# Self-attention stage of a fused transformer layer: reordering VectorE and GpSimd within a tile's pass

## What is computed

```
x = x + cross_attention(layernorm(x), context)      # context 64 x 256 x 256, 16 heads of 16
x = x + causal_self_attention(layernorm(x))         # 16 heads of 16, 64 positions
x = x + ffn(layernorm(x))                           # 256 -> 1024, ternary weights, 8-bit activations
```

```
att = softmax(where(causal, q @ k.T / 4, -inf));   y = att @ v;   x + y @ w_out + b_out
```

## Time and profile before

| | us |
|---|---|
| median of 3 runs | 949.87 |
| lowest, highest | 948.79, 952.31 |
| profiled execution, own time | 948.79 |
| profiled execution, span of the instructions | 947.0 |
| PE busy | 888.6 (94%) |
| DVE busy | 790.7 (83%) |
| ACT busy | 690.9 (73%) |
| POOL busy | 344.8 (36%) |
| mean granted TensorE clock | 0.991 |

### The profile page before, as it was taken

The page is one execution under the profiler, slowest core; times in us unless marked ns, Lnnn a source line. Parts: engine busy times, 40 slices in busy tenths (PEclk is TensorE's granted clock), DMA queues, the critical chain, the costliest instruction groups (busy, mean ns, idle before and its releaser), DMA issues. The chain is left out here.

```text
span 947.0 us, 29217 instructions
## 1 busy us (share of the span) xinstructions
PE 888.6 (94%) x9714; PEld 722.3 (76%) x9730; DVE 790.7 (83%) x1711; ACT 690.9 (73%) x1983; POOL 344.8 (36%) x487
## 2 busy tenths in 40 slices
PE   5899999999999999999999988999999987999997
PEld 4788888888888888888888876878787863555554
DVE  3788878888888888887788877988888876999997
ACT  3587776776777767777677665777777765988887
POOL 1322322223222232224322337767666632222221
PEclk9999999999999999999999999999999997999999
DMA  9111111111111111111111000000000000000001
GB/s 303 37 39 39 43 34 40 40 39 34 39 39 44 39 34 39 39 44 39 34 39 39 28 1 2 1 2 0 1 0 1 2 1 1 28 28 28 28 28 39
DMA packets 31618, 31.64 MB, mean 33 GB/s; under 512 B 3280, under 2 KB 30800, under 8 KB 31568
## 3 DMA queue, kind: packets, MB, share of 16 engines
q1 hardware_dynamic: 30720, 30.73, 10.5%
q10 hardware_dynamic: 848, 0.33, 0.1%
HBM read 26.86 MB, written 4.19 MB: 33 GB/s over the span
## 5 line engine op out<-in xcount | busy, mean ns | idle before, releaser
L485 ACT ACTIVATE probs<-psum,nmax 128x256 f32<-128x256 f32 x512 | 237.8, 488 | 89.6 <-DVE nmax L445 89.6
L445 DVE TENSOR_REDUCE nmax<-psum 128x2 f32<-128x512 f32 x256 | 159.0, 684 | 30.8 <-PE psum L315 30.8
L328 PE MATMUL psum<-id_sb,probs 128*128 128x128 f32 x1024 | 136.4, 277 | 14.3 <-ACT probs L485 14.1
L328 PEld LDWEIGHTS psum<-id_sb,probs 128*128 128x128 f32 x1024 | 111.8, 141 | 30.3 <-ACT probs L485 29.2
L493 POOL TENSOR_TENSOR rstd<-vare,minus_half 128x1 f32<-128x1 f32 x96 | 52.9, 551 | 182.2 <-DVE vare L382 179.7
L502 POOL TENSOR_TENSOR cl<-c_sb,ch 128x512 fp32r<-128x512 f32 x64 | 81.7, 1276 | 99.8 <-ACT ch L460 99.8
L485 ACT ACTIVATION_READ_ACCUMULATOR probs<-psum,nmax 128x1 f32 x512 | 112.7, 220 | 0.0
L466 ACT ACTIVATE probsT<-psum 128x512 f32<-128x512 f32 x160 | 91.0, 625 | 9.0 <-PE psum L328 8.9
L509 POOL TENSOR_TENSOR rm<-rinv,hm_sb 128x256 f32<-128x256 f32 x64 | 39.8, 622 | 127.7 <-DVE rinv L421 127.7
L315 PE MATMUL psum<-k_sb,qb 32*128 32x256 f32 x1024 | 78.4, 404 | 0.0
L1006 PE MATMUL psum<-wb_all,xqT 128*128 128x512 bf16 x240 | 66.2, 390 | 10.3 <-DVE probs L906 7.0
(11 more groups left out here) (126 smaller groups left out, 2303.5 us busy)
## 6 DMA issues: line engine op xcount, KB each, us to landing
c_sb<-in_ctx_t SPq DMA_DIRECT2D x64, 256.0 KB, 2.7
x_sb<-in_x SPq DMA_DIRECT2D x32, 128.0 KB, 2.0
out<-y_sb SPq DMA_DIRECT2D x32, 128.0 KB, 1.7
w_all<-in_w_gate SPq DMA_DIRECT2D x1, 1024.0 KB, 7.9
w_all<-in_w_up SPq DMA_DIRECT2D x1, 1024.0 KB, 10.0
w_all<-in_w_down SPq DMA_DIRECT2D x1, 1024.0 KB, 12.5
wqkv_sb<-in_w_qkv SPq DMA_DIRECT2D x1, 768.0 KB, 6.3
wq_sb<-in_wq ACTq DMA_DIRECT2D x1, 256.0 KB, 3.9
```

Of the source, the lines that this page charges most:

```text
L328: last = nc.tensor.transpose(sp[g][:, c:c + P], probs[:, 2 * g + u, kh * P:(kh + 1) * P], id_sb[:])
L445: nc.vector.tensor_reduce(nmax[:, 2 * g:2 * g + 2], sp[g].rearrange("p (u s) -> p u s", u=2), AX.X, ALU.max, negate=True).then_inc(max_don ...
L485: nc.scalar.activation(probs[:, j, :], sp[g][:, u * S:(u + 1) * S], ACT.Exp, bias=nmax[:, j:j + 1], accum_out=rsum[:, j:j + 1]).then_inc(e ...
```

## The change

Two orders are changed, both in `body2`, and no instruction is added, removed or altered. On DVE, `dve_xn` of tile t + 6 moves ahead of `dve_sum2` of tile t + 1. On POOL, `pool_kbd4` of tile t + 2 moves ahead of `pool_rm2` of tile t, and `pool_xb2` of tile t + 6 moves ahead of `pool_xl` of tile t + 5.

```diff
@@ vector engine, body2
                     if t > 0:
                         dve_y2(v, t - 1)
+                    if t + 6 < NT:
+                        dve_xn(v, LN2, t + 6, at(t + 6), xt2_mm)
                     if t + 1 < NT:
                         dve_sum2(v, t + 1)
-                    if t + 6 < NT:
-                        dve_xn(v, LN2, t + 6, at(t + 6), xt2_mm)
                     if t + 2 < NT:
                         dve_v2(v, t + 2, t % 2)
@@ gpsimd, body2
                 def body2(t):
-                    pool_rm2(p, t)
                     if t + 2 < NT:
                         n = (t + 2) // 2
                         pool_kbd4(p, t + 2, n, n % 2, t % 2)
+                    pool_rm2(p, t)
                     if t + 6 < NT:
                         pool_rstd(p, LN2, t + 6)
+                        pool_xb2(p, t + 6)
                     if t + 5 < NT:
                         pool_xl(p, t + 5, (t + 5) // 2 % 2, (t + 5) % 2)
-                    if t + 6 < NT:
-                        pool_xb2(p, t + 6)
```

## The result

The changed kernel takes 958.57 us, the median of 8 runs (954.76 to 959.84), against 950.50 for the kernel before in its 8 runs (947.75 to 952.31). The ratio is 1.0089, with a 95% interval of 1.0075 to 1.0102: slower, by about 8.5 us, where no measurable change was forecast.

A forecast was written before the change was run, and what follows sets the result against it. PE was taken to bound the self-attention stage. Profiled execution 948.79 us + 0.55 for two late passes = 949.3; with the median 1.08 higher, 950.4 was stated, range 948.5 to 953.5, no measurable change.

The forecast's parts named there:

- What bounds the kernel: Self-attention stage, 600 to 760 us: it runs at PE's pace, PE busy 159.28 of 160.00 us.
- The DVE edit: `xn` before the row sum on DVE: waits about 0.11 us for `rstd`, with 0.22 of cover left; cost zero.
- third rival: DVE becomes late if the wait before `xn` passes 0.33: 2.7 us, 952.6; chance 0.82 together with the main forecast.
- The POOL edit: POOL's order: `xb2` lands in idle time, `kbd4` goes ahead of `rm2`; the whole 1.26 us slack is spent, about zero cost.
- The sum over POOL: From the split's start to PE's `r2` load: 3.24 us, against 3.28 available, so 0.04 early.
- first rival: `rm2` becomes PE's wait at L701 in every pass: at 0.20 late, 5.4 us, 955.3; chance 0.12.
- The two single late passes: PE's `r2` load late after the splits at 586.82 and 725.40: 0.29 + 0.26 = 0.55 us.
- The slow `xn`: Three `xn` on DVE of up to 0.89 us return to 0.33 in the new place; their 0.48 us isn't counted.
- The scores start earlier: Rival: holes before L678 and L671 are waits for `kbd4`; its earlier end returns up to 6.7 us, 943.2; chance 0.06.

The follow-up runs named there:

- e7: Kernel before with PE's five hardware-loop rounds (20 passes) written out, orders and buffers as before: 947.27 us, ratio 0.9947.
- e8: Changed kernel with two `xn` buffers used in turn and PE's hardware loop written out: 946.20 us, ratio 0.9936 to the kernel before.
- e1: Kernel before with only the DVE move, `xn` ahead of the row sum; POOL's order as before: 953.99 us, ratio 1.0029.
- e6: Kernel before with only the DVE move of `xn`, plus two `xn` buffers in this stage: 951.38 us, ratio 0.9995.
- e3: Changed kernel with `kbd4` put back behind `rm2`; `xn` and `xb2` stay moved: 954.69 us, ratio 1.0038 to the kernel before.
- e4: Changed kernel with two `xn` buffers used in turn, all three moves kept: 951.74 us, ratio 0.9999 to the kernel before.
- e5: Kernel before with one move alone, `kbd4` ahead of `rm2`; `xb2` and `xn` in their old places: 967.44 us, ratio 1.0165.
- e2: Kernel before with only the POOL moves, `kbd4` ahead of `rm2` and `xb2` ahead of the split: 973.16 us, ratio 1.0233.

## Why the prediction was wrong, point by point

- *What bounds the kernel*: right. PE sets the pace of this stage; e7 and e8 show it again from the other side, since less of PE's own time shortens every pass.
- *The DVE edit, "`rstd`, which `xn` needs, ends on POOL at 710.20, so DVE now waits about 0.11 us"*: this is the step that failed. `xn` has two waits, and the second, for PE's transpose of the tile before, was left out. `dve_xn` was priced by its input alone. With that transpose's load starting 2.02 us after PE's load and its matmul ending 2.46 after it, `xn` couldn't start at 1.84. The row was there to be used: the transpose at L631 in PE's timeline. It cost about 0.75 us of DVE in every pass. The queue behind it was listed rightly and its cover (0.22 us) too; a wait of 0.77 breaks through that cover, which is the third rival's mechanism, with a wait seven times the forecast 0.11 and over twice the 0.33 that the rival set as its condition. The prediction also had no loop in it: `y2` late makes PE's transpose late, and that makes `xn` late. e1 prices it: 2.8 us. e6 takes the missed wait away, and the step as written holds: `xn` starts 1.84 after the load, DVE's idle time before L733 falls from 0.33 to about 0.2, and the ratio is 0.9995.
- *The POOL edit, "`xb2` lands in what is now POOL's idle time and leaves the pair behind it"*: wrong in consequence. `xb2` waits for `xn`, and with `xn` at 2.53 it pushes the split, `kbd4` and `rm2`. `kbd4` ahead of `rm2` had used up the slack of 1.26 us, so nearly all that the split is late (0.42 us) is PE's (0.35 a pass). That is the rest of the loss, from e3's 1.0038 to 1.0089.
- *The sum over POOL, 3.24 us from the split to PE's load*: right. In the changed kernel it is 716.55 - 713.34 = 3.21, and in e4 it fits under 3.28 with no wait. In the kernel written out it fits under 6.42 too. So the first rival, that `kbd4` makes `rm2` late whatever `xn` does, had the right symptom (PE waits at L701, passes over 6.7 us) and the wrong cause: e4 has the same order and no such wait. Without `xn`'s and `xb2`'s move it is true, as e5 and e2 show.
- *The two single late passes, 0.55 us*: the changed kernel can't show them, since every pass is late; e4 can. The first was there and smaller: PE's load at 592.95 waits 0.18 us for `rm`, where 0.29 was counted. The second was not: apart from the first, every split in e4 stands at least 3.26 us ahead of the load. In all, e4's passes add to what they were in the kernel before within 0.2 us.
- *The slow `xn`*: right that they go, wrong on 0.33. In the changed kernel all 23 in the steady stretch take 0.41 us, none 0.89. The new place gives 0.41 in e1, e3, e4, e6 and e8 too, against 0.33 behind the reciprocal; why is not tested. The slow ones stay with the old place: three in the steady stretch of the kernel before and eleven in e7, each starting within 0.06 us of POOL's split, and none in e6 or e8. The Trainium skill ("SBUF — State Buffer", "Who interferes with whom") says that VectorE in its two-port mode and GpSimd can't hold the shared ports together and that the one which starts second is blocked. That fits the meeting of the two; which one started first these rows can't tell, since `xn` and the split stand at 744.68 both. It bore on the DVE time only, which had cover.
- *The scores start earlier*: no. The holes before L678 are 5.2 us in 23 passes after and 5.4 in 24 before, though `kbd4` moved.

That PE's transpose follows `y2` is shown by its start. In the hardware loop's passes it comes 0.63 or 0.64 us after the start of `y2` in all but a few passes of every kernel, in e1 too, where `y2` itself is late; in written-out passes it comes 0.48 after it, and where it has to wait there the profile names L760 (e1, e7). So a wait that the profile calls "issue" was in part a wait for DVE, and the prediction had taken "issue" for no engine.

What stays open: no kernel without the transpose's wait for `y2` was tried, since the two results share a bank; e6 breaks the loop at its other end. The kernel before with two `xn` buffers and no move was not run either; its steady passes never wait for the one buffer.

## What to carry to other kernels

When an instruction is moved forward, look up every wait in front of it, above all the one on whoever reads its output buffer: an order in which that wait is always over leaves no row in the steady passes, so it must be priced from the reader's timeline. A single buffer between two engines turns "earlier" into a round trip; a second buffer makes the same move free. And where one move spends all of a slack, price it together with whatever can shift its start, not by itself.

## What the runs showed that I had not expected

- Moves that cost can cost less together: `kbd4` alone 1.0165, all three 1.0089. Moving `xn` costs by itself (e1), but with the other two moves in place it shortens the pass from 7.40 (e2) to 6.92 us, since `xb2` gets its `xn` earlier. Moving `xb2` ahead of the split takes 0.7 us out of the chain that `kbd4` lengthens, if `xn` is early enough (e4), and puts 0.2 more into it if it is not (e2).
- PE's hardware loop costs 0.15 us a pass and 0.25 more at each jump in this stage. The 0.15 lies in one place: from the start of `y2` to PE's transpose it is 0.64 us in the loop and 0.48 written out, and the rest of the pass is the same. Written out, the stage is 4.0 us shorter from the first L701 to the last (e7; the ratio of 0.9947 is 5 us of 950).
